# A convolution and mixture-of-experts block whose inputs are laid out by the host

## What is computed

```python
# convolution part
m = pat                                           # 3 x 3 mask
quant_weight(w): t = tanh(w); t = t / (2 * max|t|) + 0.5; return 2 * round(15 * t) / 15 - 1
y = _ln_c(x)
c1 = conv3x3(quant_act(batchnorm(y, gamma1, beta1)), quant_weight(w1) * m)
c2 = conv3x3(quant_act(batchnorm(c1, gamma2, beta2)), quant_weight(w2) * m)
x = x + c2 + y
# mixture of experts: 16384 tokens, 8 experts, two for each token, 682 hidden
t = tokens(x)
z = _ln_t(t)
gates = top2(softmax(z @ router_w.T)), normalised
out = t + sum over e of gates[:, e] * ((silu(z @ ew1[e].T) * (z @ ew3[e].T)) @ ew2[e].T)
```

## Time and profile before

| what | us |
|---|---|
| median of 3 runs | 840.13 (839.19 to 841.62) |
| span of the profiled execution | 838.0 |
| TensorE busy | 774.5 |
| VectorE busy | 562.4 |
| ScalarE busy | 491.8 |
| GpSimd busy | 540.8 |

### The profile page before, as it was taken

One profiled execution on the slowest core, in us unless ns is written; L12 is line 12 of the kernel. 1 busy time (PEld: TensorE's weight loads), 2 busy tenths in 40 slices (PEclk: granted clock), 3 DMA queues, 4 the chain that ended last, 5 costly groups with the idle time before them and its releaser, 6 DMA issues.

```text
span 838.0 us, 17914 instructions
## 1 busy us (share of the span) xinstructions
PE 774.5 (92%) x5003; PEld 444.2 (53%) x5007; DVE 562.4 (67%) x1462; ACT 491.8 (59%) x1071; POOL 540.8 (65%) x564
## 2 busy tenths in 40 slices
PE   8979978886899999999999999999999999999834
PEld 6744465564354545454545455454545457777523
DVE  5976678888566666666666666666767566666445
ACT  5836458775166666666666666666666566666400
POOL 3520027777777777777777777777777777777610
PEclk9969989897999999999999999999999999999955
DMA  8760023343244443333334343433333346666179
GB/s 197 138 111 1 0 62 102 115 136 110 80 131 134 123 122 115 112 116 112 114 113 121 108 124 106 129 112 116 113 114 115 104 134 183 185 180 185 62 273 327
DMA packets 84227, 105.55 MB, mean 126 GB/s; under 512 B 27061, under 2 KB 57966, under 8 KB 84176
## 3 DMA queue, kind: packets, MB, share of 16 engines
q1 hardware_dynamic: 60688, 79.27, 32.5%
q0 software_dynamic: 19136, 21.54, 9.1%
q10 hardware_dynamic: 4352, 4.20, 1.5%
HBM read 73.90 MB, written 27.30 MB: 121 GB/s over the span
## 4 chain that ended last, share of the span: by engine, by line
PE 80%; DVE 8%; issue 4%; DMA 3%; SPq 2%; ACT 2%; DVEq 0%; POOL 0%; POOLq 0%; ACTq 0%
PE bank L1432 40%; PE bank L1447 22%; PE bank L1312 6%; PE bank L1413 3%; DMA conv_all<-result_rows 2%; PE bank L1405 2%; SPq L492 1%; PE bank L1234 1%; PE bank L1247 1%; PE bank L1252 1%; PE bank L1263 1%; PE bank L1337 1%; PE bank L1330 1%; DMA x_all<-in_x 1%; DVE stats L1011 1%
## 5 line engine op out<-in xcount | busy, mean ns | idle before, releaser
L553 POOL DMA_INDIRECT expert_rows<-y_and_rows,slot_all x256 | 249.4, 974 | 144.2 <-issue 77.1
L1165 DVE TENSOR_TENSOR conv_all<-conv_all,bank 128x512 f32<-128x512 f32 x340 | 233.6, 688 | 151.5 <-ACT conv_all L747 149.2
L1432 PE MATMUL bank<-xT,w 64*128 64x512 f32 (+1 forms) x1608 | 324.7, 534 | 0.4 <-DVE conv_all L1165 0.4
L747 ACT ACTIVATE conv_all<-bank 128x512 f32<-128x512 f32 x340 | 203.2, 598 | 117.0 <-PE bank L1432 117.0
L1432 PEld LDWEIGHTS bank<-xT,w 64*128 64x128 f32 x1608 | 143.7, 185 | 170.3 <-DVE conv_all L1165 86.2
L563 POOL DMA_INDIRECT result_rows<-conv_all,dest_all x142 | 140.1, 987 | 47.1 <-issue 40.9
L1447 PE MATMUL bank<-conv_all,w 128*64 128x256 f32 x1240 | 161.7, 384 | 1.2 <-DVE tile_map L1134 1.2
L1447 PEld LDWEIGHTS bank<-conv_all,w 128*64 128x64 f32 x1240 | 91.1, 136 | 51.7 <-issue 12.7
L758 ACT ACTIVATE xT<-bank 64x256 f32<-64x256 f32 x272 | 103.3, 380 | 18.6 <-PE bank L1405 16.2
L765 ACT ACTIVATE conv_all<-bank 128x256 f32<-128x256 f32 x68 | 26.2, 385 | 85.6 <-PE bank L1447 85.6
L563 POOL DMA_INDIRECT result_rows<-squares,dest_all x64 | 63.2, 987 | 19.5 <-issue 18.6
(11 more groups left out here) (247 smaller groups left out, 882.9 us busy)
## 6 DMA issues: line engine op xcount, KB each, us to landing
w<-expert_w SPq DMA_DIRECT2D x68, 384.0 KB
w<-expert_w SPq DMA_DIRECT2D x68, 192.0 KB
conv_all<-expert_rows SPq DMA_DIRECT2D x56, 136.0 KB
x_all<-in_x SPq DMA_DIRECT2D x16, 256.0 KB, 4.0
x_all<-y_and_rows POOLq DMA_DIRECT2D x16, 256.0 KB, 4.3
expert_rows<-y_and_rows,slot_all POOLq DMA_INDIRECT x256
y_and_rows<-result_rows SPq DMA_DIRECT2D x8, 512.0 KB, 10.2
conv_all<-result_rows SPq DMA_DIRECT2D x8, 512.0 KB, 11.0
```

The lines of the kernel that those rows point to most:

```text
L553: nc.gpsimd.indirect_dma_start(xs, bass.IndirectOffsetOnAxis(ap=slot_all[:, s, k * GH + g:k * GH + g + 1], axis=0), rows_all[:, s, g, :], ...
L747: nc.scalar.activation(sbuf[k % 3], h1_ps[k % 3][:], ACT.Silu).then_inc(silu_rdy, 1)
L1165: V.tensor_tensor(hbuf[k], sbuf[k % 3], h3_ps[k % 3][:], ALU.mult).then_inc(mul_rdy, 1)
L1432: ins = mm(ps[k % 3][:, rows_], w[half, cols], xT[u][half, rows_], start=True, stop=True)
```

## The change

The host lays the inputs out before the launch, and the output after it.

- `x` comes as 8 blocks [128, 1024], contiguous; the output leaves in the same form. One DMA a pair over 128 partitions with pieces of 4 KB.
- Convolution weights come as [in, tap, out], both layers, and repeated for both halves of the partitions: [128, 2 x 576]. Tanh, maximum and levels work on 128 partitions. The mask multiply on GpSimd writes the block-diagonal `wblk` straight, in four instructions (two layers, two halves of the partitions). `levels` 4 and 5, `turn_conv_weights` and `blocks` go. The zeroing of `wblk` moves to the end of GpSimd's zeroing, with a wait of its own.
- Expert weights come turned, stacked and padded as `w13` and `w2t`; `stack_weights`, the ScalarE copies, the loads and stores on SP and the tensors `wsc` and `w2sc` go. Tiles load from `w13` and `w2t`.
- `gamma` and `beta` come as one [128, 4].

```diff
-                for h in range(2):
-                    sp.dma_start(xb[64 * h:64 * h + 64, 2 * S * p:2 * S * (p + 1)]
-                                 .rearrange("c (i p) -> c i p", i=2 * IMG), xv[h, p]).then_inc(x_in[p % 2], 16)
+                sp.dma_start(xb[:, 2 * S * p:2 * S * (p + 1)], x[p]).then_inc(x_in[p % 2], 16)
                 if p == 0:
-                    for k, w in enumerate((w1, w2)):
-                        sp.dma_start(wc[:, k, :], w.rearrange("o i a b -> o (i a b)")).then_inc(wc_in, 16)
+                    sp.dma_start(wc[:].rearrange("p l n -> p (l n)"), conv_w).then_inc(wc_in, 16)
...
-            for t in (chosen, rwt, wblk, *qpad):
-                ins = nc.gpsimd.memset(t[:], 0.0)
-            ins.then_inc(zero_p, 1)
+            for t in (chosen, rwt, *qpad):
+                nc.gpsimd.memset(t[:], 0.0)
+            made(nc.gpsimd.memset(wblk[:], 0.0))
+            pool.sem_inc(zero_p, 1)
...
             pool.wait_ge(wq_rdy, 4)
-            wv = wc[:].rearrange("o k (i t) -> o (k i) t", t=TAPS)
-            nc.gpsimd.tensor_tensor(wv, wv, patf[:].unsqueeze(1).broadcast_to([C, 2 * C, TAPS]),
-                                    ALU.mult).then_inc(wmask_rdy, 1)
+            for l in range(2):
+                for h in range(2):
+                    rows_ = slice(C * h, C * h + C)
+                    ins = nc.gpsimd.tensor_tensor(wblk[rows_, l, :, C * h:C * h + C],
+                                                  wc[rows_, l, :].rearrange("i (t o) -> i t o", t=TAPS),
+                                                  patf[rows_, :].unsqueeze(2).broadcast_to([C, TAPS, C]), ALU.mult)
+            ins.then_inc(wb_rdy, 1)
...
-                if p < 6:
+                if p < 4:
                     levels(p)
-            act.wait_ge(zero_p, 1)
-            blocks(0)
-            blocks(1)
...
-                for h in range(2):
-                    nc.scalar.dma_start(outv[h, p], xb[64 * h:64 * h + 64, 2 * S * p:2 * S * (p + 1)]
-                                 .rearrange("c (i p) -> c i p", i=2 * IMG)).then_inc(o_out, 16)
+                nc.scalar.dma_start(out[p], xb[:, 2 * S * p:2 * S * (p + 1)]).then_inc(o_out, 16)
...
-                if p >= NP - 2:
-                    turn_conv_weights(p - NP + 2)
-
-            pe.wait_ge(wb_rdy, 2)
+
+            pe.wait_ge(wb_rdy, 1)
...
             def route(p, first=False, last=0):
-                stack_weights(p)
```

More of the change, by code:

```diff
@@ L26, with conv_moe_kernel @@
 NOT_CHOSEN = -1e30
-def conv_moe_kernel(nc, x, gamma1, beta1, w1, gamma2, beta2, w2, pat, router_w, ew1, ew2, ew3, out):
-    N, C, H, W = x.shape
-    E, HID, _ = ew1.shape
+def conv_moe_kernel(nc, shape, x, gamma_beta, conv_w, pat, router_w, w13, w2t, out):
+    N, C, H, W = shape
+    E, HID = router_w.shape[0], 682
     HW = H * W
@@ L394, in _ @@
                          pad_rows[:]).then_inc(dummy_out, 16)
[L396 to L425, removed]
             sp.wait_ge(dummy_out, 16)
             sp.wait_ge(tmap_rdy, 1)
-            sp.wait_ge(w_out, 32 * E)
             def scattered(stripes):
@@ L582, in _ @@
             act.sem_inc(y_sb, 1)
[L583 removed]
+            act.wait_ge(wc_in, 16)
             nc.scalar.activation(wc[:], wc[:], ACT.Tanh).then_inc(th_rdy, 1)
@@ L620, in levels @@
                     ins = nc.scalar.activation(wc[:], wc[:], ACT.Copy, bias=-ROUND)
-                elif n == 3:
+                else:
                     act.wait_ge(wq_rdy, 3)
                     ins = nc.scalar.activation(wc[:], wc[:], ACT.Copy, bias=-LEVELS, scale=2.0)
-                else:
-                    k = n - 4
-                    act.wait_ge(wmask_rdy, 1)
-                    for d in range(2):
-                        ins = nc.scalar.activation(wdup[:, k, :, d, :],
-                                                   wc[:, k, :].rearrange("o (i t) -> o t i", t=TAPS), ACT.Copy)
-                ins.then_inc(wq_rdy, 1)
-            def blocks(k):
-                act.wait_ge(wT_rdy, k + 1)
-                turned = w_bf[k].rearrange("p (t c) -> p t c", t=TAPS)
-                nc.scalar.activation(wblk[0:64, k, :, 0:64], turned[0:64], ACT.Copy)
-                nc.scalar.activation(wblk[64:128, k, :, 64:128], turned[64:128], ACT.Copy).then_inc(wb_rdy, 1)
+                ins.then_inc(wq_rdy, 1)
             square(0, 0)
@@ L709, in route @@
                         affine(1, 2 * p + 4 + u, u)
-                if not first:
-                    wait_apart(act, w_out, 32 * p)
-                for b in range(2):
-                    n = min(512, WST - 512 * b)
-                    act.wait_ge(wt_ps, 3 * p + b + 1)
-                    nc.scalar.activation(wstk[:, 512 * b:512 * b + n], w_bank(b)[:, 0:n],
-                                         ACT.Copy).then_inc(wt_sb, 1)
-                act.wait_ge(wt_ps, 3 * p + 3)
-                nc.scalar.activation(w2s[:, 0:HT, :].rearrange("p k c -> p (k c)"), w_bank(2)[:, 0:HT * C],
-                                     ACT.Copy)
-                nc.scalar.activation(w2s[0:HR, HT, :], w_bank(2)[0:HR, HT * C:KT * C],
-                                     ACT.Copy).then_inc(wt_sb, 1)
                 tokens(p)
@@ L1491 @@
     nc = bacc.Bacc("TRN2", target_bir_lowering=False, num_devices=1)
+    laid = layouts(*(np.asarray(inputs[name]) for name in _INS))
     arrays, args = {}, []
-    for name in _INS:
-        a = np.ascontiguousarray(inputs[name])
+    for name, a in laid.items():
+        a = np.ascontiguousarray(a)
         arrays[f"in_{name}"] = a
         args.append(nc.dram_tensor(f"in_{name}", a.shape, mb.dt.from_np(a.dtype), kind="ExternalInput").ap())
-    shape = inputs['x'].shape
-    args.append(nc.dram_tensor("out_0", shape, mb.dt.from_np(np.dtype("float32")), kind="ExternalOutput").ap())
-    conv_moe_kernel(nc, *args)
+    N, C, H, W = inputs['x'].shape
+    args.append(nc.dram_tensor("out_0", (N // 8, 2 * C, 4 * H * W), mb.dt.from_np(np.dtype("float32")),
+                               kind="ExternalOutput").ap())
+    conv_moe_kernel(nc, (N, C, H, W), *args)
     r = run_bass_kernel_spmd(nc, [arrays], core_ids=[0])
-    return r.results[0]["out_0"]
+    o = r.results[0]["out_0"].reshape(N // 8, 2, C, 4, H, W)
+    return np.ascontiguousarray(o.transpose(1, 0, 3, 2, 4, 5).reshape(N, C, H, W))
```

105 lines of the change are left out of this document (37 added, 68 removed).

## The result

The median after is **846.52 us** (840.28 to 849.44, 14 executions) against 839.66 (837.16 to 842.29, 14) for the kernel before, taken beside it: ratio 1.008, 95% interval 1.0062 to 1.0097. The change makes the kernel slower by 6.9 us. The prediction said 839.2, in a range that ended at 843.3. The profiled execution after has a span of 845.7 us, 7.7 more than that of before.

What follows compares the result with a forecast made beforehand. TensorE was taken to bound the expert tiles, with GpSimd almost as close; changes elsewhere summed to -0.9 us on the 838.0 span, 837.1, plus 2.1 for the median: 839.2 us, 8-in-10 range 836.0 to 843.3.

Steps and rivals of the forecast that it cites:

- part 4's term for the clock: Routing loop: without the transposes one more route in four chances has its convolution at half clock, +0.3 us (-1.3 to +5).
- the clock in routing: Rival: the clock falls in all four other routes with a convolution, 1.3 us each, +5, giving 843.9; chance 0.09.
- part 4 as a whole: Routing without on-chip expert-weight stacking: mostly covered by VectorE; -0.8 for a wait in route 6, +0.3 for the clock.
- The longest quiet stretch doesn't grow: Routing: argument against more clock falls, that TensorE's longest quiet stretch, from turning to convolution, stays as long.
- The 0.84 us at L984: Route 6: VectorE's wait for exponentials queued behind ScalarE's removed copies goes, -0.8 us.
- Part 1: Inputs at the start: with larger loads, TensorE's 0.53 us wait for the second pair of x goes, -0.5 us.
- Part 2: Mask in the norm: four GpSimd multiplies hold VectorE steps, +2.6 us; a clock fall behind them, +0.6.
- Part 3: Norm: convolution-weight copies and turns go, -0.2 and -1.8 us; the latter at most -2.5, where VectorE is next.
- Part 5: End: last stores faster, -1.0 us (-0.4 to -1.3); loads and stores mixing, -0.1 (-0.8 to +2.6 if stores go ahead).
- VectorE isn't held: Rival, mask: GpSimd's multiplies do not hold VectorE a second time, so 2.6 and 0.6 drop out, 836.0 us; chance 0.11.
- the multiplies are slow: Rival, mask: GpSimd takes twice 2.16 ns per element, +5.0 us, giving 844.2; chance 0.05.
- The early half clock: Rival, start: TensorE's half clock goes once there is no idle time at 9 us, -1.8, giving 837.4; chance 0.05.

Runs made afterwards that it cites:

- filler ahead of positions: Kernel after with six filling matmuls of 512 columns before the positions in routes 1 to 7: 839.16 us, ratio 0.9967.
- dummy turns: Kernel after with twelve transposes of the identity, read by nobody, put into each route: 839.33 us, ratio 0.9979.
- both fillers: Kernel after with filling matmuls, either six before positions (routes 1 to 7), 839.16 us, or eight between convolution and turning (routes 0 to 5), 837.97 us.
- Part 4 alone: Kernel before with only the expert weights stacked by the host, everything else unchanged: 842.38 us, ratio 1.0026.
- the other parts: Kernel after with the expert weights turned and stacked on the chip again: 837.35 us, ratio 0.9973.
- gentler mask: Kernel after with filler in all routes, mask multiplied in place by two GpSimd instructions over 128 partitions, ScalarE copying the blocks: 832.15 us, ratio 0.991.

## Why the prediction was wrong

**The step that failed is part 4's term for the clock, +0.3** ("for one more such route in four chances"). The mechanism was among the rivals, the clock in routing, at 0.09; the rows bore it out and its price was too small as well. The rival had four more falls at 1.3 us, 843.9 in all. From the first reduction of the routes to the last the kernel after took 9.05 us more, where part 4 as a whole was to give 0.5 back; with the 0.84 us that did go, the clock cost about 9.9 us for the 0.3. The runs show:

- *How often.* The clock fell in all six routes. "The longest quiet stretch doesn't grow" was the argument against. It did grow: the longest idle piece in a route of the loop was 1.59 us before and 1.93 to 2.00 after, and up to 2.52 in the runs with filler ahead of positions. And it was the wrong thing to ask: the clock held over an idle piece of 2.50 us in one route with filler, and fell behind one of 1.93 without. What the runs decide is only that with more work for TensorE in the route, whatever it computes, more convolutions ran at full clock. The prediction took the transposes for covered by VectorE and costed their removal at nothing; nobody waited for them, but they kept the clock up.
- *What one costs.* In the steps 2-3 and 3-4 1.25 us, as worked out. But step 1-2 lost 3.4 us, where VectorE waited for both stripes of the convolution (1.72 and 1.81 us), and 6-7 lost 2.1, with 0.87 and 1.96, and that after the 0.84 us of L984 had been saved in it. A fall that lands on the turning of rows, in the filler runs, costs 0.3 to 0.6 us.

That the lost TensorE work is the cause, and neither the copies nor the DMAs, is shown by the dummy turns and by both fillers. How the clock comes to fall in one route and not in the next is not shown. The 0.84 us at L984 went as forecast: L895 follows the choice at once.

**Part 1** held. The second pair is there without a wait (the centring of both pairs runs in one piece, first line), loads ran at 311 GB/s from 2 to 10 us against 221, and GpSimd's multiplies start 0.55 us earlier than the one of before.

```profile
6.12 4.47 PE L1158 MATMUL bank<-x_all,centre_half 128*128 128x512 f32 x8
```

```profile
DMA packets 813, 2.49 MB, mean 311 GB/s; under 512 B 224, under 2 KB 224, under 8 KB 813
```

**Part 2**: right mechanism, sizes off both ways, and a sum that is right by luck. From the first multiply's start to the end of the wide copy it is 5.31 us against 3.68 before: +1.6 in place of +2.6. A multiply takes 1.19 us rather than 1.25, and a held VectorE step ends with it, so that the steps add no time between the multiplies as I had assumed. The clock behind it cost more: the next centring took 3.33 us in place of 1.88, +1.5 for +0.6. Both together +3.1 against +3.2 forecast. In the six other traces with four multiplies that centring took 2.50 to 3.62 us, in all three with two multiplies 1.88, and mending the mask gained 2.4 to 2.9. The Trainium skill (SBUF — State Buffer, section Who interferes with whom) has VectorE and GpSimd lock each other out for a whole instruction, and counts copies in a two-port mode among those it concerns. The trace agrees on the first, since three small steps with two inputs end as a multiply ends. The wide copy, with one input, was held too, 1.69 us for its usual 0.69, which fits the second; no run here shows which mode that copy was in.

**Part 3**: turn and copies went, the router's turn no longer waits for ScalarE, and the gain was larger than forecast. Ten filling matmuls ran from 53.15 in 3.56 us, where nine had taken 4.05, and ended at 56.7. VectorE had the moments at 56.9, 2.1 us later than before, as parts 1 and 2 had delayed it. So the pairing now followed VectorE, which is the case that the prediction gave as the limit of part 3: -2.5 and not -1.8. With the +2.1 of the delay (forecast with parts 1 and 2 and the -0.2: +2.5) that is the -0.4 measured, against a forecast of +0.7 for the norm. It became -0.9 at the second convolution, since the eighteen filling matmuls behind the pairing took 4.04 us where they had taken 4.65. These are readings of one trace; over all traces of that code the pairing came 1.1 us earlier than over those of the code before.

**Part 5**: from the last sum's end to the end of the span 3.1 us in place of 4.8, -1.7 for -1.0 and outside the bounds given. Against it the loads: the last addition comes 25.2 us after the first, not 23.7, +1.5 for -0.1. Pieces of 1 KB bring that from 24.3 to 23.3 in one pair of kernels and from 24.1 to 23.2 in another, and the tail behind the last sum from 3.1 to 3.4 us. Over all traces it is 23.7 to 25.5 us with pieces of 4 KB (eight), 23.2 and 23.3 with pieces of 1 KB over 128 partitions, and 23.1 to 23.7 with the stores of before (three). In the first pair, from 803 to 828 us, a store of 4 KB pieces landed 6.1 us after its issue in the median, one of 1 KB pieces 9.4 us. So some 1.0 of the 1.5 is larger pieces that let stores go ahead of loads, the case that the prediction bounded at +2.6; the rest lies within the spread of the traces. The two sizes cancel: -0.2 for -1.1. The Trainium skill (DMA: Bandwidth & Descriptors, section Queues, rings and completion order) has a DMA engine take turns between its queues by packets; that larger packets of stores would then take more of it is inferred from that, and these spans agree.

Of the other rivals, that VectorE isn't held and that the multiplies are slow are refuted by the rows above. The early half clock lessened but did not go: the granted clock is 0.50 from 15 to 17 us in both traces, and the four passes from 13.34 took 2.47 us where those from 13.88 had taken 3.24.

With the transposes' work given back, the kernel stands where the forecast had it: 839.3 us with dummy turns, 839.2 with filler. That is luck in part, since the terms of parts 2, 3 and 5 were off and cancel.

**What stays open.** Part 4 alone costs 2.2 us in the median, but 9.2 on top of the other parts (846.5 against 837.4). The profiled execution of its upper half, 843.5 to 845.6, looks as the kernel after does. Of the kernel after thirteen of fourteen executions took 844.4 us or more, with a granted clock of 0.926 to 0.932, and one took 840.28, with 0.941. How many executions fall into the train of slow routes may hang on small shifts ahead of the routing; that is not shown, and what sets it wasn't found. Nor is it shown why the slow convolutions shorten by 0.3 us from route to route.

## What to carry to other kernels

Before taking work from an engine that isn't the bound, look at the granted clock of the stretch: where it is already below 1 in some rounds of a loop, the work to be removed may be what keeps it up, and its removal must be priced by rounds at the lower level. If it goes all the same, put filling matmuls in its place, and read not only how many rounds still fall but on what: on the convolution a fall cost 1.25 us and up to 3.4, on the turning of rows 0.3 to 0.6. Where two chains meet at one instruction, write down both arrival times after the whole change; which of them came last is what decided part 3 here.

## What the runs showed of the hardware

- Twelve transposes of the identity a route, read by nobody, made the kernel 7.2 us faster. With filler, the gentler mask and stores of 1 KB a loss of 6.9 us is a gain of 8.6.
- Filler without the transposes did not end the falls of the clock but moved most of them off the convolutions: with filler and the gentler mask four routes turned their rows in 3.3 to 3.7 us for 2.05, and every convolution took 4.21. With transposes and filler together no fall was left between 123 and 200 us.
- GpSimd multiplies and VectorE steps took turns one by one: four multiplies of 64 partitions by 576 elements held three small VectorE steps and one copy, one each. Two over 128 partitions (in f32 in place, the four wrote bf16 elsewhere) do the same work in 2.26 us in place of 4.76: 1.13 us each against 1.19, so the time went by the elements in a partition, not by the partitions.
- Stores in pieces of 4 KB finish 0.3 us sooner than in pieces of 1 KB, but delay the loads beside them by about 1 us in 24.
